# The first k tiles of a fused attention and feed-forward kernel: maxima ahead of transposes, half of the first moves on GpSimd, key sums in their usual beats

## Chip, cores and metric

The kernel runs on one core of a Trainium2 chip. The metric is the device time of one execution in microseconds (us), lower is better. Engines are named as in the profile: PE is TensorE, PEld its weight loads, DVE is VectorE, ACT is ScalarE, POOL is GpSimd, SP is SyncE (it only issues transfers here); a q behind a name (SPq, POOLq) means the engine's queue.

## What is computed

For each of 16 batch items, x is 128 rows by 1024 columns and ctx is the same size. Cut to what matters here:

```python
q = layernorm(x); k = v = ctx
qh = softmax(Wq @ q, over the 64 rows of a head) * 64 ** -0.5
kh = softmax(Wk @ k, over the 1024 columns)        # 8 heads x 64 rows = 4 tiles of 128 rows
context = kh @ vh.T                                # per head, 64 x 64
out = Wo @ (context.T @ qh) + bo
x = x + out / norm(out) * g * sqrt(128)
# then a feed-forward part with a router over 256 slots (aux_keys, aux_values, Wvd, Wvu, Wr)
rk = aux_keys @ Wr.T;  values = aux_values @ Wvd.T # tables, once per call
```

## The kernel before

The attention part is a hand-written software pipeline. A loop `for b in range(PERIODS)` runs over periods, and each engine has its own copy of it with its instructions written out in order; semaphores join the engines. In period b the k side of item b is made (four k tiles, `k_tile(b, i)`, i = 0 to 3, called k(b,i) below), the q side of item b-1 (`q_pair`, `q_shift`, `q_turn`), and the output of item b-2 (`o_pair`). The four values of i are the beats of a period.

One k tile goes through the engines so. PE makes it in PSUM with six products (each operand is split in a high and a low part, so `ctx_hi`, `ctx_lo`, `xn_hi`, `xn_lo` have to be there first). DVE takes its maximum (`k_maximum`, tile `nkm`), ACT takes the exponential (`k_exponential`, `ek`), DVE transposes it in 32 x 32 blocks (`k_turn`, `kt`). In period 0 the tiles use two PSUM places in turn, `k_slot` and `q_slot`, so k(0,2) waits for the exponential of k(0,0) and k(0,3) for that of k(0,1); later k tiles share `k_slot` alone, and k(1,0) waits for the exponential of k(0,3).

When two tiles of an item are transposed, 16 small transfers of 64 KB (`move_k(b, half)`, SBUF to SBUF, 32 partitions by 2 by 256 elements each) put the blocks in `ekT`. PE then sums keys times context over 8 steps (`g_part(b, half, ...)` into `gm`), ACT copies the sum (`g_copy`), PE multiplies by the head products (`m_product`), ACT scales (`mt_scale`).

The q side: `q_pair(b, i)` makes two row blocks in `q_slot`; DVE takes maxima (`qm`) and subtracts (`qs_sb`), ACT takes the exponential, DVE sums (`qsum`) and inverts (`qrec`), POOL multiplies (`q_scale`), PE transposes (`q_turn`), ACT copies. `q_pair` of item b also needs `x_low(b)` from POOL. The layernorm of item b takes statistics on DVE (`x_statistics`), a power on POOL (`rstd_pow`), a bias on DVE (`x_bias`, tile `nb`), then ACT (`x_layernorm`, `x_high`) and POOL (`x_low`).

The router tables come by five transfers that POOL issues once, and PE makes two sets of products of them: `value_products` (16 short products, which the trace counts as 32, and one of the router) and `score_product`. DVE order in period 0 is: maximum of tile i-1, transpose of tile i-1, maximum of tile i, so the maximum of a tile stands behind the transpose of the one before.

Of the kernel before, what the change touches and what calls it, by code (L numbers as in the profile page):

```python
# [47 lines left out]
def attention_ffn_kernel(nc, x, ctx_rows, ctx_cols, WqT_raw, WkT_raw, Wv_rows, WoT_rows, bo_row, g_col, Wuq_cols,  # L48
# [3 lines left out]
    with ctx:  # L52
# [207 lines left out]
        k_T = sem("k_T")  # L260
        k_moved = [sem(f"k_moved{k}") for k in range(2)]
        krec_done = sem("krec_done")
        kscale_done = sem("kscale_done")
# [84 lines left out]
        def has(b):  # L348
            return 0 <= b < B

        @block.sync
        def _(sp):
# [12 lines left out]
            def move_k(b, half):  # L365

                sp.wait_ge(k_T, 4 * b + 2 * half + 2)
                wait(sp, g_prod, 2 * (b - 1) + half + 1)
                for q in range(QUAD):
                    for a in range(QUAD):  # L370
                        sp.dma_start(ekT[q * BLK:(q + 1) * BLK, 2 * half:2 * half + 2, a, :],
                                     kt[a * BLK:(a + 1) * BLK, 2 * half:2 * half + 2,
                                        q * J * BLK:(q + 1) * J * BLK]).then_inc(k_moved[half], 16)
# [24 lines left out]
            for half in range(2):  # L398
                sp.wait_ge(k_moved[half], MOVED * B)
            sp.dma_start(Wuq_in[:, :, :], Wuq_cols).then_inc(wuq_in, 16)  # L400
# [24 lines left out]
        def _(pe):  # L425
# [33 lines left out]
            def g_part(b, half, js):  # L459

                if js[0] == 0:
                    pe.wait_ge(k_moved[half], MOVED * (b + 1))
                    if half == 0:
                        pe.wait_ge(ctxT_in[b % 2], 16 * (b // 2 + 1))
                        wait(pe, mt_copied, b)
                cols = slice(half * 2 * P, (half + 1) * 2 * P)
                for j in js:
                    last = nc.tensor.matmul(gm[:, cols], ctxT[:, b % 2, j, :], ekT[:, 2 * half:2 * half + 2, :, j * BLK:(j + 1) * BLK],  # L468
                                            start=(j == 0), stop=(j == J - 1))
                if js[-1] == J - 1:  # L470
                    last.then_inc(g_prod, 1)
# [37 lines left out]

            def value_products():  # L510
                pe.wait_ge(table_in, 16 * TABLES)
                for s in range(NSLOT // P):
                    for j in range(J):
                        last = nc.tensor.matmul(ob[:, s * VB:(s + 1) * VB], valuesT[:, j, s * P:(s + 1) * P],
                                                WvdT[:, j, :], start=(j == 0), stop=(j == J - 1))
                last.then_inc(vv_prod, 1)
                nc.tensor.matmul(ob[0:RDIM, NSLOT:2 * NSLOT], WrT, keysT, start=True, stop=True).then_inc(rk_prod, 1)

# [87 lines left out]
            for b in range(PERIODS):  # L606
                p, o, e = b - 1, b - 2, b - 3
                for i in range(4):
                    if has(b):
                        k_tile(b, i)  # L610
                    qb, qi = (p, i - 2) if i >= 2 else (o, i + 2)
                    if has(qb):
                        if qb == 0 and qi == 0:
                            pe.wait_ge(u_done, 1)
                            pe.wait_ge(ident_in, 16)
                        take_turn(q_turn, qb, qi)
                        q_turn(qb, qi)
# [83 lines left out]
        def _(act):  # L701
# [102 lines left out]
            for weights, raw, come, done in ((WkT, WkT_in, k_weights_in, k_weights),  # L804
# [3 lines left out]
                if weights is WkT:  # L808
                    ctx_high(0)
            x_layernorm(0)  # L810
            x_high(0)
            for b in range(PERIODS):
                p, o, e = b - 1, b - 2, b - 3
                for i in range(4):
# [7 lines left out]
                    if has(qb):  # L822
                        q_exponential(qb, qi)
                    if has(b):
                        k_exponential(b, i)
                    if i == 1 and has(b + 1):
                        ctx_high(b + 1)
# [12 lines left out]
                    if i == 2:  # L840
                        if has(p) and p > 0:
                            g_copy(p)
                        if 0 < b < B:
                            x_high(b)
                    if b == 1 and i == 0:
                        act.wait_ge(u_prod, 1)
                        nc.scalar.copy(U[:, :, :].rearrange("p h c -> p (h c)"), turn[:, :]).then_inc(u_done, 1)
                    if b == 1 and i == 3:
                        g_copy(0)
                        act.wait_ge(vv_prod, 1)  # L850
                        nc.scalar.copy(VV[:, :, :].rearrange("p s (r d) -> p s r d", d=VB),
                                       ob[:, 0:2 * VB].rearrange("p (s d) -> p s d", d=VB).unsqueeze(2).broadcast_to(
                                           [P, NSLOT // P, P // VB, VB])).then_inc(vv_copied, 1)
                        act.wait_ge(rk_prod, 1)
# [4 lines left out]
                    if b == 2 and i == 0:  # L859
                        act.wait_ge(b1_prod, 1)  # L860
# [5 lines left out]
                    if b == B and i == 3:  # L866
                        for half in range(2):
                            act.wait_ge(k_moved[half], MOVED * B)
                        h_scale(0, 0)
# [50 lines left out]
        def _(pool):  # L920
# [52 lines left out]
            nc.gpsimd.memset(scoreB[BOT:P, :], 0.0).then_inc(score_zeros, 1)  # L973
            pool.wait_ge(score_zeros, 1)
            rstd_pow(0)
            x_low(0)
            ctx_low(1)
            nc.gpsimd.dma_start(valuesT, values_cols).then_inc(table_in, 16)
            nc.gpsimd.dma_start(WvdT, Wvd_cols).then_inc(table_in, 16)
            nc.gpsimd.dma_start(keysT, keysT_raw).then_inc(table_in, 16)  # L980
            nc.gpsimd.dma_start(WrT, WrT_raw).then_inc(table_in, 16)
            nc.gpsimd.dma_start(Wr_in, Wr_raw).then_inc(table_in, 16)
            for n in range(2):
                nc.gpsimd.dma_start(scoreB[BOT:BOT + 1, n * NSLOT:(n + 1) * NSLOT], log_rel_row).then_inc(log_rel_in, 16)
            for b in range(PERIODS):
                p, o, e = b - 1, b - 2, b - 3
                for i in range(4):
# [15 lines left out]
                    if b == B and i == 3:  # L1003
                        for half in range(2):
                            pool.wait_ge(k_moved[half], MOVED * B)
                        nc.gpsimd.memset(q_rows[:, :, BOT:P], 1.0).then_inc(query_ones, 1)
# [29 lines left out]
        def _(dve):  # L1036
# [21 lines left out]
            def k_turn(b, i):  # L1058
                dve.wait_ge(k_exp, 4 * b + i + 1)
                wait(dve, k_moved[i // 2], MOVED * b)  # L1060
                V.transpose(kt[:, i, :], ek[:, i % 2, :]).then_inc(k_T, 1)  # L1061
# [144 lines left out]
            def hidden_step(b):  # L1206
                if b == 0:
                    dve.wait_ge(ffn_in, 16 * FFN_DMAS)
                    for half in range(2):
                        dve.wait_ge(k_moved[half], MOVED * B)  # L1210
                    hT_low(0, 0)
# [37 lines left out]
            weights_low(WqT, WqT_in, q_weights)  # L1249
            x_bias(0)  # L1250
            for b in range(PERIODS):
                p, o, e = b - 1, b - 2, b - 3
                for i in range(4):
                    kb, ki = (b, i - 1) if i else (p, 3)
                    if has(kb):
                        k_turn(kb, ki)
                    if has(b):
                        k_maximum(b, i)
# [130 lines left out]
```

## Time and profile before

| what | value |
|---|---|
| median of 3 runs | 663.33 us (662.93 to 663.96) |
| the profiled execution, its own time | 663.27 us |
| its span, first to last instruction | 661.5 us |
| PE busy | 625.1 us, 95% |
| DVE busy | 579.0 us, 88% |
| ACT busy | 419.5 us, 63% |
| POOL busy | 366.4 us, 55% |

The span is 1.8 us shorter than the time of the same execution; the difference lies outside the first and last instruction. Busy shares are averages over the attention part, the feed-forward part and the two ends, so they don't say what holds any one stretch.

### The profile page before, as it was taken

What the parts mean: (1) busy time and instruction counts of PE and PEld (TensorE: products, weight loads), DVE (VectorE), ACT (ScalarE), POOL (GpSimd) and SP (SyncE); (2) the same over time, 40 slices, a digit from 0 to 9 for tenths busy, and PEclk for the clock granted to TensorE, in tenths of its full rate; (3) what the DMA queues carried; (4) which work ended last, traced back from release to release, by engine and by line L of the source; (5) the groups of instructions that cost most, each with busy time, mean ns of one, the idle gap of its engine ahead of it and who ended that gap; (6) DMA issues with size and microseconds to landing.
All of it is one profiled execution on the core that took longest, in us unless ns stands there. A gap on an engine that the chain in (4) does not pass through costs nothing.

```text
span 661.5 us, 11769 instructions
## 1 busy us (share of the span) xinstructions
PE 625.1 (95%) x3974; PEld 546.4 (83%) x3974; DVE 579.0 (88%) x788; ACT 419.5 (63%) x844; POOL 366.4 (55%) x275
## 2 busy tenths in 40 slices
PE   4699999999999999999999999999999799999896
PEld 2487888888888888888888888888889799998574
DVE  4697899999999999999999999999997656866897
ACT  4355676666666666666666766666573856584784
POOL 2434355565655647464646565656546576752294
PEclk9799999999999999999999999999999899999898
DMA  7644244434434343434343434443234100000056
GB/s 262 190 122 121 81 143 112 144 86 143 124 100 133 102 133 102 135 96 136 101 136 104 133 97 134 123 130 97 65 101 148 41 1 2 1 1 1 33 209 268
DMA packets 52779, 72.57 MB, mean 110 GB/s; under 512 B 10112, under 2 KB 43424, under 8 KB 52464
## 3 DMA queue, kind: packets, MB, share of 16 engines
q1 hardware_dynamic: 52336, 70.43, 35.6%
q0 software_dynamic: 384, 1.40, 0.7%
q8 instruction: 32, 0.52, 0.4%
q14 instruction: 27, 0.22, 0.1%
HBM read 29.85 MB, written 8.39 MB: 58 GB/s over the span
## 4 chain that ended last, share of the span: by engine, by line
PE 45%; DVE 29%; issue 19%; ACT 3%; DMA 2%; SPq 2%; POOL 1%; DVEq 0%; ACTq 0%; POOLq 0%
PE gm L468 9%; DVE qm L1075 7%; DVE qsum L1085 7%; PE ob L491 6%; PE gm L542 4%; PE turn L542 4%; DVE nkm L1056 3%; DVE qs_sb L1078 3%; DVE st L1042 3%; DVE st L1100 3%; PE q_slot L428 2%; PE turn L499 2%; DVE kt L1061 2%; PE k_slot L428 2%; PE k_slot L430 2%
## 5 line engine op out<-in xcount | busy, mean ns | idle before, releaser
L942 POOL TENSOR_TENSOR qs_sb<-qs_sb,qrec 128x1024 f32<-128x1024 f32 x64 | 122.0, 1907 | 211.6 <-DVE qrec L1089 211.6
L723 ACT ACTIVATE ek<-k_slot,nkm 128x1024 f32<-128x1024 f32 x62 | 69.1, 1114 | 104.4 <-DVE nkm L1056 104.4
L491 PE MATMUL ob<-mt_sb,q_hd 128*128 128x128 f32 x1024 | 127.3, 278 | 3.7 <-POOL mt_sb L948 3.1
L491 PEld LDWEIGHTS ob<-mt_sb,q_hd 128*128 128x128 f32 x1024 | 122.5, 193 | 8.4 <-issue 3.5
L468 PE MATMUL gm<-ekT,ctxT 128*128 128x256 f32 x512 | 118.2, 379 | 0.0
L468 PEld LDWEIGHTS gm<-ekT,ctxT 128*128 128x128 f32 x512 | 97.0, 190 | 14.8 <-DMA ekT<-kt 0.3
L733 ACT ACTIVATE qs_sb<-qs_sb 128x1024 f32<-128x1024 f32 x64 | 68.5, 1070 | 42.4 <-DVE qs_sb L1078 42.4
L1056 DVE TENSOR_REDUCE nkm<-k_slot 128x1 f32<-128x1024 f32 x62 | 74.2, 1197 | 17.6 <-PE k_slot L430 17.6
L1061 DVE STREAM_TRANSPOSE kt<-ek 128x1024 f32<-128x1024 f32 x64 | 78.6, 1228 | 5.8 <-ACT ek L723 5.8
L1085 DVE TENSOR_REDUCE qsum<-qs_sb 128x16 f32<-128x1024 f32 x64 | 76.9, 1202 | 5.2 <-ACT qs_sb L733 5.2
L1078 DVE TENSOR_TENSOR qs_sb<-q_slot,qm 128x1024 f32<-128x1024 f32 x64 | 78.4, 1225 | 2.2
L1075 DVE TENSOR_REDUCE qm<-q_slot 128x16 f32<-128x1024 f32 x64 | 75.3, 1177 | 0.0
L428 PE MATMUL k_slot<-ctx_hi,WkT_hi 128*128 128x512 f32 x124 | 55.1, 445 | 13.1 <-DVE ctx_lo L1246 7.4
L454 PE MATMUL turn<-ident,qs_sb 128*128 128x128 f32 x512 | 66.3, 273 | 0.0
L454 PEld LDWEIGHTS turn<-ident,qs_sb 128*128 128x128 f32 x512 | 59.6, 141 | 7.8
L738 ACT COPY q_hd<-turn 128x1024 f32<-128x1024 f32 x64 | 64.3, 1005 | 2.0 <-PE turn L454 2.0
L428 PE MATMUL q_slot<-WqT_hi,xn_hi 128*128 128x512 f32 x128 | 55.8, 436 | 6.1 <-DVE qs_sb L1078 5.2
L429 PE MATMUL q_slot<-WqT_hi,xn_lo 128*128 128x512 f32 x128 | 50.6, 396 | 0.0
L430 PE MATMUL q_slot<-WqT_lo,xn_hi 128*128 128x512 f32 x128 | 50.6, 396 | 0.0
L430 PE MATMUL k_slot<-ctx_lo,WkT_hi 128*128 128x512 f32 x124 | 50.1, 404 | 0.0
L429 PE MATMUL k_slot<-ctx_hi,WkT_lo 128*128 128x512 f32 x124 | 49.6, 400 | 0.0
L968 POOL TENSOR_TENSOR x_all<-x_all,hbuf 128x1024 f32<-128x1024 f32 x16 | 38.7, 2428 | 9.8 <-ACT hbuf L770 9.8
(195 smaller groups left out, 1270.7 us busy)
## 6 DMA issues: line engine op xcount, KB each, us to landing
ekT<-kt SPq DMA_DIRECT2D x512, 64.0 KB, 2.0
ctx_in<-ctx_rows SPq DMA_DIRECT2D x16, 512.0 KB, 4.6
x_all<-x SPq DMA_DIRECT2D x16, 512.0 KB, 3.6
ctxT<-ctx_cols SPq DMA_DIRECT2D x16, 512.0 KB, 4.0
out<-q_hd SPq DMA_DIRECT2D x15, 512.0 KB, 2.6
Wuq_in<-Wuq_cols SPq DMA_DIRECT2D x1, 1280.0 KB, 5.4
x_all<-values_cols POOLq DMA_DIRECT2D x1, 1024.0 KB, 6.1
WvuT_in<-WvuT_raw SPq DMA_DIRECT2D x1, 512.0 KB, 4.6
```

The costliest lines, as they stand in the source:

```text
L428: nc.tensor.matmul(dst, lhs[0], rhs[0], start=True, stop=False)
L429: nc.tensor.matmul(dst, lhs[1], rhs[0], start=False, stop=False)
L430: return nc.tensor.matmul(dst, lhs[0], rhs[1], start=False, stop=True)
L454: last = nc.tensor.transpose(turn[:, (2 * t + n) * P:(2 * t + n + 1) * P], qs_sb[:, i % 2, n * HALF + t * P:n * HALF + (t + 1) * P], ident ...
L468: last = nc.tensor.matmul(gm[:, cols], ctxT[:, b % 2, j, :], ekT[:, 2 * half:2 * half + 2, :, j * BLK:(j + 1) * BLK], start=(j == 0), stop ...
L491: last = nc.tensor.matmul(ob[:, (j % 4) * C:(j % 4 + 1) * C], q_hd[:, t, j * P:(j + 1) * P], mt_sb[:, b % 2, t, :], start=(t == 0), stop=( ...
L942: nc.gpsimd.tensor_tensor(e, e, qrec[:, i % 2, :].unsqueeze(2).broadcast_to([P, PAIR, DH]), ALU.mult).then_inc(q_mul, 1)
L1056: V.tensor_reduce(nkm[:, i:i + 1], k_psum(b, i)[:, :], AX, ALU.max, negate=True).then_inc(k_max, 1)
L1061: V.transpose(kt[:, i, :], ek[:, i % 2, :]).then_inc(k_T, 1)
L1075: V.tensor_reduce(qm[:, :], q, AX, ALU.max).then_inc(q_max, 1)
L1078: V.tensor_tensor(qs_sb[:, i % 2, :].rearrange("p (m d) -> p m d", d=DH), q, qm[:, :].unsqueeze(2).broadcast_to([P, PAIR, DH]), ALU.subtra ...
L1085: V.tensor_reduce(qsum[:, :], qs_sb[:, i % 2, :].rearrange("p (m d) -> p m d", d=DH), AX, ALU.add).then_inc(q_sum, 1)
```

## The change

On DVE the four maxima and three of the four transposes of item 0 are written ahead of the loop, each maximum ahead of the transpose of the tile before. ACT's first exponentials stand between the layernorm, `ctx_high(1)` and `x_high(0)`. POOL issues the table transfers first, then makes `ctx_low(1)` and `x_low(0)`, then issues 8 of the 16 moves of each half of item 0; SP issues the other 8. The key sums of item 0 (`g_part`) go to the beats that all other items have, the value products are split in two and moved ahead, and the copies of the tables on ACT are moved with them.

```diff
 sync:    def move_k(b, half):
                 for q in range(QUAD):
-                    for a in range(QUAD):
+                    for a in range(QUAD // 2 if b == 0 else QUAD):
 tensor:  def g_part(b, half, js):
-                    pe.wait_ge(k_moved[half], MOVED * (b + 1))
+                    pe.wait_ge(k_moved[half], moved(b + 1))
+                    if b == 0:
+                        pe.wait_ge(k_moved_first[half], MOVED // 2)
...
+                    if b == 1 and i == 1:
+                        value_products(1)
+                        router_product()
...
-                        if p == 0 and i == 1:
-                            g_part(p, 0, range(0, 8))
-                        if p == 0 and i == 3:
-                            g_part(p, 1, range(0, 8))
+                        if p == 0 and i == 0:
+                            value_products(0)
-                        if p > 0 and i == 1:
-                            g_part(p, 0, range(4, 8))
-                        if p > 0 and i == 2:
+                        if i == 1:
+                            g_part(p, 0, range(4 if p > 0 else 0, 8))
+                        if i == 2:
                             g_part(p, 1, range(0, 8))
...
                     if b == 1 and i == 2:
-                        value_products()
-                    if b == 1 and i == 3:
                         score_product()
 scalar:      x_layernorm(0)
+            k_exponential(0, 0)
+            ctx_high(1)
+            k_exponential(0, 1)
             x_high(0)
+            k_exponential(0, 2)
+            k_exponential(0, 3)
...
                     if i == 2:
-                        if has(p) and p > 0:
+                        if has(p):
                             g_copy(p)
...
-                    if b == 1 and i == 3:
-                        g_copy(0)
-                        act.wait_ge(vv_prod, 1)
+                    if b == 1 and i == 1:
+                        act.wait_ge(vv_prod, NSLOT // P)
+                        act.wait_ge(rk_prod, 1)
 gpsimd:
+            def move_k(half):
+                pool.wait_ge(k_T, 2 * half + 2)
+                for q in range(QUAD):
+                    for a in range(QUAD // 2, QUAD):
+                        nc.gpsimd.dma_start(ekT[...], kt[...]).then_inc(k_moved_first[half], 16)
             rstd_pow(0)
-            x_low(0)
-            ctx_low(1)
             (five table transfers)
+            ctx_low(1)
+            x_low(0)
+            for half in range(2):
+                move_k(half)
             (two transfers of log_rel)
 vector:      x_bias(0)
+            k_maximum(0, 0)
+            for i in range(1, 4):
+                k_maximum(0, i)
+                k_turn(0, i - 1)
```

In the rows of instruction order below, the line numbers of before and after differ, since the file has grown. On DVE at the start of the program, `nkm` is a k tile's maximum and `kt` its transpose. Before:

```order
L1056 TENSOR_REDUCE nkm<-k_slot 128x1
L1061 STREAM_TRANSPOSE kt<-ek 128x1024
L1056 TENSOR_REDUCE nkm<-q_slot 128x1
L1061 STREAM_TRANSPOSE kt<-ek 128x1024
L1056 TENSOR_REDUCE nkm<-k_slot 128x1
```

And now, at the same place on DVE:

```order
L1078 TENSOR_REDUCE nkm<-k_slot 128x1
L1078 TENSOR_REDUCE nkm<-q_slot 128x1
L1085 STREAM_TRANSPOSE kt<-ek 128x1024
L1078 TENSOR_REDUCE nkm<-k_slot 128x1
L1085 STREAM_TRANSPOSE kt<-ek 128x1024
```

The second maximum has gone ahead of the first transpose, and so on down the four tiles. On POOL at the start of the program (DMA is the issue of a transfer), before:

```order
L932 TENSOR_TENSOR rstd<-ve,half_neg 128x1
L936 TENSOR_TENSOR xn_lo<-xn,xn_hi 128x1024
L923 TENSOR_TENSOR ctx_lo<-ctx_in,ctx_hi 128x1024
L978 DMA x_all<-values_cols 128x2048
L979 DMA x_all<-Wvd_cols 128x512
L980 DMA x_all<-keysT_raw 64x256
L981 DMA x_all<-WrT_raw 64x48
L982 DMA x_all<-Wr_raw 48x64
L984 DMA scoreB<-log_rel_row 1x16x16 x2
L930 TENSOR_SCALAR ve<-mv 128x1
```

And now on POOL:

```order
L944 TENSOR_TENSOR rstd<-ve,half_neg 128x1
L996 DMA x_all<-values_cols 128x2048
L997 DMA x_all<-Wvd_cols 128x512
L998 DMA x_all<-keysT_raw 64x256
L999 DMA x_all<-WrT_raw 64x48
L1000 DMA x_all<-Wr_raw 48x64
L935 TENSOR_TENSOR ctx_lo<-ctx_in,ctx_hi 128x1024
L948 TENSOR_TENSOR xn_lo<-xn,xn_hi 128x1024
L991 DMA ekT<-kt 32x2x256 x16
L1006 DMA scoreB<-log_rel_row 1x16x16 x2
L942 TENSOR_SCALAR ve<-mv 128x1
```

The two subtractions changed places and stand behind the tables, and 16 issues of moves stand ahead of the power for item 1's layernorm (`ve<-mv`). On PE, from the end of the q pair of beat 2 of period 1 to k(1,3), before:

```order
L430 MATMUL q_slot<-WqT_lo,xn_hi 128x512
L514 MATMUL ob<-x_all 128x64 x16
L517 MATMUL ob<-x_all 48x256
L428 MATMUL k_slot<-ctx_hi,WkT_hi 128x512
L429 MATMUL k_slot<-ctx_hi,WkT_lo 128x512
```

And now the same part of period 1 on PE (`ob<-x_all 128x64` are the value products, `48x256` the router's, `64x256` the score product, `gm` the key sums):

```order
L436 MATMUL q_slot<-WqT_lo,xn_hi 128x512
L476 MATMUL gm<-ekT,ctxT 128x256 x8
L531 MATMUL ob<-x_all 64x256
L434 MATMUL k_slot<-ctx_hi,WkT_hi 128x512
L435 MATMUL k_slot<-ctx_hi,WkT_lo 128x512
```

The second half of the key sums now stands ahead of k(1,3), where the value products were; those stand around k(1,1), eight products ahead of it and eight behind.

## Rows read from the trace of the kernel before

**Rows 1.** Chain of work that ended last: start us, us, engine, tile, line.

```profile
42.57 3.52 PE ob L514 x32
46.09 0.56 PE ob L517 x2
...
54.62 1.09 PE gm L477 x16
...
104.34 3.45 PE gm L468 x16
```

**Rows 2.** Stretches, each engine's busy us, PEclk the granted clock.

```profile
24.00:27.00 3.00, 2.23 (x5) 1.82 (x6) 1.25 (x1) 0.63 (x2) 0.58 (x2) 0.50 0.95 342
...
56.00:86.00 30.00, 30.00 (x192) 26.12 (x191) 26.08 (x29) 19.26 (x36) 11.38 (x9) 1.00 0.33 90
```

**Rows 3.** Timeline of period 0: start us, us, engine line op, then idle before.

```profile
10.38 1.23 DVE L1056 TENSOR_REDUCE nkm<-k_slot 128x1 f32<-128x1024 f32 x1 [0.16 <-PE k_slot L430]
...
12.27 0.63 PE L430 MATMUL q_slot<-ctx_lo,WkT_hi 128*128 128x512 f32 x1
12.55 1.11 ACT L723 ACTIVATE ek<-k_slot,nkm 128x1024 f32<-128x1024 f32 x1
...
13.78 1.25 DVE L1061 STREAM_TRANSPOSE kt<-ek 128x1024 f32<-128x1024 f32 x1 [2.17 <-ACT ek L723]
...
13.89 0.47 PE L428 MATMUL k_slot<-ctx_hi,WkT_hi 128*128 128x512 f32 x1 [0.99 <-ACT ek L723]
...
14.95 1.19 DVE L1056 TENSOR_REDUCE nkm<-q_slot 128x1 f32<-128x1024 f32 x1
...
24.77 0.76 PE L428 MATMUL k_slot<-ctx_hi,WkT_hi 128*128 128x512 f32 x1 [4.54 <-ACT ek L723]
```

**Rows 4.** Timeline: issues of transfers on the queues of SP and POOL.

```profile
8.24 0.43 SPq L384 DMA_DIRECT2D ident<-identity  x1
...
18.68 10.60 SPq L371 DMA_DIRECT2D ekT<-kt  x16
...
20.69 0.81 POOL L978 DMA_DIRECT2D x_all<-values_cols  x1
...
22.04 0.56 POOL L980 DMA_DIRECT2D x_all<-keysT_raw  x1
```

**Rows 5.** Transfers of the first 60 us: KB each, median us from issue to landing.

```profile
ekT<-kt SPq DMA_DIRECT2D x57, 64.0 KB, 2.0
...
x_all<-keysT_raw POOLq DMA_DIRECT2D x1, 64.0 KB, 6.3
```

**Rows 6.** Timeline of period 1, first half, DVE and one PE row.

```profile
27.70 1.22 DVE L1056 TENSOR_REDUCE nkm<-k_slot 128x1 f32<-128x1024 f32 x1 [1.80 <-PE k_slot L430]
...
36.55 1.87 DVE L1051 SCALAR_TENSOR_TENSOR nb<-mv,rstd 128x1 f32<-128x1 f32 x1
...
39.59 1.23 DVE L1078 TENSOR_TENSOR qs_sb<-q_slot,qm 128x1024 f32<-128x1024 f32 x1
...
40.96 0.47 PE L428 MATMUL q_slot<-WqT_hi,xn_hi 128*128 128x512 f32 x1 [0.74 <-DVE qs_sb L1078]
```

**Rows 7.** Timeline from beat 3 of period 1 into period 2.

```profile
46.58 0.50 PE L428 MATMUL k_slot<-ctx_hi,WkT_hi 128*128 128x512 f32 x1
...
48.08 1.03 PE L454 MATMUL turn<-ident,qs_sb 128*128 128x128 f32 x8
...
48.28 1.22 DVE L1056 TENSOR_REDUCE nkm<-k_slot 128x1 f32<-128x1024 f32 x1 [0.30 <-PE k_slot L430]
...
48.87 0.48 PE L428 MATMUL q_slot<-WqT_hi,xn_hi 128*128 128x512 f32 x1
...
50.33 3.61 PE L468 MATMUL gm<-ekT,ctxT 128*128 128x256 f32 x16
...
52.85 2.36 POOL L936 TENSOR_TENSOR xn_lo<-xn,xn_hi 128x1024 fp32r<-128x1024 f32 x1
...
58.51 0.48 PE L428 MATMUL q_slot<-WqT_hi,xn_hi 128*128 128x512 f32 x1
```

More of the change, by code:

```diff
@@ L261, in attention_ffn_kernel @@
         k_moved = [sem(f"k_moved{k}") for k in range(2)]
+        k_moved_first = [sem(f"k_moved_first{k}") for k in range(2)]
         krec_done = sem("krec_done")
@@ L349, in has, with moved @@
             return 0 <= b < B
+        def moved(b):
+            return MOVED * b - MOVED // 2 if b else 0
         @block.sync
@@ L398, in _ @@
             for half in range(2):
-                sp.wait_ge(k_moved[half], MOVED * B)
+                sp.wait_ge(k_moved[half], moved(B))
             sp.dma_start(Wuq_in[:, :, :], Wuq_cols).then_inc(wuq_in, 16)
@@ L508, in head_products, with value_products, router_product @@
                 last.then_inc(u_prod, 1)
-            def value_products():
+            def value_products(s):
                 pe.wait_ge(table_in, 16 * TABLES)
[L512 to L515, printed above, removed]
+                for j in range(J):
+                    last = nc.tensor.matmul(ob[:, s * VB:(s + 1) * VB], valuesT[:, j, s * P:(s + 1) * P],
+                                            WvdT[:, j, :], start=(j == 0), stop=(j == J - 1))
                 last.then_inc(vv_prod, 1)
+            def router_product():
                 nc.tensor.matmul(ob[0:RDIM, NSLOT:2 * NSLOT], WrT, keysT, start=True, stop=True).then_inc(rk_prod, 1)
@@ L823, in _ @@
                         q_exponential(qb, qi)
-                    if has(b):
+                    if 0 < b < B:
                         k_exponential(b, i)
-                    if i == 1 and has(b + 1):
+                    if i == 1 and 0 < b and has(b + 1):
                         ctx_high(b + 1)
@@ L853, in _ @@
                                            [P, NSLOT // P, P // VB, VB])).then_inc(vv_copied, 1)
-                        act.wait_ge(rk_prod, 1)
                         nc.scalar.copy(rkT, ob[0:RDIM, NSLOT:2 * NSLOT]).then_inc(rk_copied, 1)
@@ L858, in _ @@
                                       float(BOT) ** -0.5).then_inc(score_ready, 1)
-                    if b == 2 and i == 0:
+                    if b == 1 and i == 3:
                         act.wait_ge(b1_prod, 1)
@@ L867, in _ @@
                         for half in range(2):
-                            act.wait_ge(k_moved[half], MOVED * B)
+                            act.wait_ge(k_moved[half], moved(B))
                         h_scale(0, 0)
@@ L974, in _ @@
             pool.wait_ge(score_zeros, 1)
+            def move_k(half):
+                pool.wait_ge(k_T, 2 * half + 2)
+                for q in range(QUAD):
+                    for a in range(QUAD // 2, QUAD):
+                        nc.gpsimd.dma_start(ekT[q * BLK:(q + 1) * BLK, 2 * half:2 * half + 2, a, :],
+                                            kt[a * BLK:(a + 1) * BLK, 2 * half:2 * half + 2,
+                                               q * J * BLK:(q + 1) * J * BLK]).then_inc(k_moved_first[half], 16)
             rstd_pow(0)
-            x_low(0)
-            ctx_low(1)
             nc.gpsimd.dma_start(valuesT, values_cols).then_inc(table_in, 16)
@@ L1004, in _ @@
                         for half in range(2):
-                            pool.wait_ge(k_moved[half], MOVED * B)
+                            pool.wait_ge(k_moved[half], moved(B))
                         nc.gpsimd.memset(q_rows[:, :, BOT:P], 1.0).then_inc(query_ones, 1)
@@ L1059, in k_turn @@
                 dve.wait_ge(k_exp, 4 * b + i + 1)
-                wait(dve, k_moved[i // 2], MOVED * b)
+                wait(dve, k_moved[i // 2], moved(b))
+                if b == 1:
+                    dve.wait_ge(k_moved_first[i // 2], MOVED // 2)
                 V.transpose(kt[:, i, :], ek[:, i % 2, :]).then_inc(k_T, 1)
@@ L1209, in hidden_step @@
                     for half in range(2):
-                        dve.wait_ge(k_moved[half], MOVED * B)
+                        dve.wait_ge(k_moved[half], moved(B))
                     hT_low(0, 0)
@@ L1254, in _ @@
                     kb, ki = (b, i - 1) if i else (p, 3)
-                    if has(kb):
+                    if has(kb) and b > 0:
                         k_turn(kb, ki)
-                    if has(b):
+                    if 0 < b < B:
                         k_maximum(b, i)
```

## The prediction

> **What bounds the kernel now.** I read the chain of work that ended last first. From about 42 us on it runs through PE for two periods and keeps coming back to it: value products, key sums, head products [rows 1]. The table of stretches says the same of period 2: in the 30.00 us from 56 to 86, PE is busy for all 30.00 and DVE for 26.08, so PE holds and DVE waits [rows 2]. So what counts is how early PE gets into period 2 and how early the k and q chains feed it; from there on, as long as nothing else is late, every microsecond won at the start is won at the end. The timeline of period 0 shows a different picture: there the tiles go round one by one. A tile's maximum stands behind the transpose of the tile before (13.78, then 14.95) although its product was finished at 12.27 + 0.63 = 12.90 [rows 3], and PE sits idle for 4.54 us ahead of k(1,0) at 24.77 [rows 3]. The stretch that follows has a granted clock of 0.50 [rows 2], that is 1.2 GHz of the levels 1.2 and 2.4.
>
> **Period 0, step by step.** Four handovers are read from rows 3: maximum to exponential 1.22 (10.38 + 1.23, about when the next may start), exponential to transpose 13.78 - 12.55 = 1.23, exponential to the next k tile on PE 13.89 - 12.55 = 1.34, transpose to what follows on DVE 14.95 - 13.78 = 1.17 [rows 3]; what follows a maximum on DVE starts 1.12 later (27.70 to the next at 28.85 is 1.15). A k tile's maximum starts 48.28 - 46.58 = 1.70 after the tile [rows 7]. Maximum 0 stays at 10.38, and exponential 0 moves to 11.60, since ACT's cast goes behind it. Maximum 1 starts at 12.94, when its product is done. k(0,2) starts at 11.60 + 1.34 = 12.94. DVE: transpose 0 at 14.06, maximum 2 at 15.23, transpose 1 at 16.35, maximum 3 at 17.51, transpose 2 at 18.63. ACT: exponential 1 at 12.94 + 1.22 = 14.16, 2 at 16.45, 3 at 18.73; the casts `ctx_high(1)` and `x_high(0)`, about 1 us each, lie in the holes between and cost nothing (12.8 to 13.8, and 15.4 to 16.4); without those holes each would cost its 1 us. Transpose 3 follows at about 20.0, and k(1,0) starts at 18.73 + 1.34 = 20.07 in place of 24.77: **4.7 us** earlier. PE's idle time ahead of it falls from 4.54 to about 2 us. A gap of that size in period 0 (idle between k(0,2) and k(0,3)) was not followed by a fall of the clock, so I count k(1,0) and the first q pair at 2.4 GHz. If the clock fell all the same, the 12 products at 1.2 GHz would cost up to 2.3 us more.
>
> **POOL's queue.** This is the part with a price that the trace doesn't show. `rstd_pow(0)` ends near 10.0, five table issues follow (0.81 for the first, 0.56 for the others [rows 4]) to about 13.0, `ctx_low(1)` is done at 16.3 and `x_low(0)` at 16.5 + 2.4 = 18.9, both ahead of 20.07. The tables have from about 12.5 to 23 us to land. Then come 16 issues of moves of unknown price p, two issues for `log_rel` (about 1.0 together) and the power (0.9): item 1's `rstd` is ready at 20.75 + 16p. Behind it wait DVE's `nb`, and behind that all of DVE. For p the nearest row is the issue of `keysT_raw`, also 64 KB and also 64 runs of 1 KB: 0.56 [rows 4]. The far bounds are 0.81, the dearest POOL issue, and 0.56 x 0.66/0.43 = 0.86, if this shape costs POOL as much more as it costs SP: 10.60/16 = 0.66 for a move, 0.43 for the 64 KB of `ident` [rows 4]. I take 0.56, by likeness of the transfer: `rstd` at 29.7. DVE takes the maximum of k(1,0) at 20.07 + 1.70 = 21.8 and reaches `nb` 36.55 - 27.70 = 8.85 later [rows 6], at 30.6. So 0.9 us is in hand, and `nb` costs nothing extra. With 0.81 or 0.86 DVE waits 3.1 or 3.9 us.
>
> The same rows bear on contention: beside the table issues, from 21.0 to 23.4, DVE did a transpose and a maximum, and the issue in their midst kept its 0.56 [rows 4]. So I count no hindrance. If DVE's transposes and statistics between 19 and 29 us (four instructions or pairs, 1.25 for a transpose [rows 3]), did hold POOL up for their length, `rstd` would come 5 us later.
>
> The Trainium skill ("SBUF — State Buffer", the warning on the DVE that blocks DMA, section "SBUF: two separate sides") states that GpSimd cannot write descriptors while a DVE instruction in a two-port mode holds the port pair they share. If the transposes and statistics were of that kind, that would be the case of the 5 us; the trace's 0.56 beside a transpose speaks against it.
>
> **Landing of the moves.** DVE wants half 0 moved for the transpose of k(1,0), PE for the key sums. SP issues its 8 of half 0 from 17.6 (end of transpose 1) to 22.9, POOL its 8 from 18.9 to 23.3. Landing takes 2.0 at the median for a move, 6.3 for POOL's 64 KB table [rows 5]; that one stood behind a table of 1 MB on the same queue, and nothing of that size is ahead of the moves now, so I take 3. Half 0 is there at about 26. The transpose is due at 26.7 and the key sums at 30: nothing lost. With 6.3 it is there at 29.1, a DVE wait of 2.4. Half 1 is issued by 28.8 on SP and 27.8 on POOL and wanted at 37 or later.
>
> **Period 1 on PE.** Now it should run almost without a hole. From k(1,0) to k(1,3) stand three k tiles at 1.50, three q pairs at 1.46, one transpose at 0.79 [rows 7], two key sums at 3.45, the value products at 3.52, router and score product at 0.56 each [rows 1]: 4.50 + 4.38 + 0.79 + 6.90 + 3.52 + 1.12 = 21.2, so k(1,3) starts at 41.3. Waits that could break it: q pair 2 needs the subtraction of pair 1, 3.04 behind `nb` plus 1.37 [rows 6], 30.6 + 4.4 = 35.0, and PE comes there at 35.8, so 0.8 us in hand; the value products wait for the tables, landed; the key sums for the moves, landed; ACT's copies of the tables (1.1 us together) stand behind the layernorm that ends near 33.6 and ahead of an exponential due at 34.9, so they just fit.
>
> **What is given back.** The next q pair (item 1, pair 0) needs `x_low(1)` on POOL, and that follows k(1,3)'s maximum by way of DVE's sum and POOL's scaling: from the maximum to the end of `x_low`, 52.85 + 2.36 - 48.28 = 6.93 [rows 7]. So this pair starts at 41.3 + 1.70 + 6.93 = 49.9. PE itself would be there at 41.3 + 1.5 + 0.8 + 1.5 + 1.1 (`m_product` [rows 1]) + 1.5 + 0.8 = 48.4; 1.5 us of PE's lead is lost to POOL. Before, the same pair started at 58.51 [rows 7]. 58.5 - 49.9 = 8.6, and I count **8.5 us**: 4.7 from period 0, 5.3 from holes and slow products in period 1, 1.5 given back. DVE is then ahead by about 8.8, SP's moves by 5 or more where they had slack, so none of them is the later one, and PE keeps the lead through period 2, which had no hole [rows 2]. Against the profiled execution: 663.27 - 8.5 = **654.8**; the median of before is within 0.1 of it.
>
> **The rivals.** (1) *POOL's issues are dear.* A wait w of DVE at `nb` reaches PE as w - 0.8. With p = 0.81 the gain is 8.5 - 2.3 = 6.2, time 657.1; with 0.86, 657.9; with 5 us of hindrance by DVE, w = 5.0 - 0.9 = 4.1, 658.1 (0.04 of the chance). For it: the move is of a shape that costs SP half as much again. Against: the 64 KB row at 0.56. (2) *Moves land late:* DVE waits 2.4 at the transpose of k(1,0), 2.4 - 0.8 = 1.6 pass on: 656.4. For it: 6.3 us in rows 5, and two queues now move at once; against: no 1 MB ahead. (3) *The clock:* slow products at k(0,2) cost 0.6 and at k(1,0) up to 2.3: 655.4 to 657.1. (4) *Slower than before:* the issues of moves hold POOL so long that the power for item 1 comes later than all that was won. That needs w - 0.8 over 8.5, w = 9.3, so 20.75 + 16p = 39.9, p = 1.2. At p = 1.3, w = 10.95 and the time is 663.3 + 1.6 = 664.9. The dearest issue in sight is 0.86, so the chance is small. (5) *The later beats don't gain:* only period 0's 4.7 arrives because ACT's copies or the value products delay the q chain as much as the holes were worth: 658.6. Against: the slack of 0.8 and 1.3 us worked out above. (6) *Absorbed:* were DVE or SP the bound of the later periods, little would come through; rows 2 speak against it, time 662 to 663.3.
>
> **How the numbers follow.** Forecast as summed 0.56; (1) 0.20; (2) 0.07; (3) 0.06; (4) 0.03; (5) 0.04; (6) 0.04. The forecast alone has a range of 653.7 to 656.0, from handovers that are good to 0.1 each over some ten steps. To hold 8 in 10, the range takes in (1) up to 0.86 with some blocking, (2), (3) and (5): 653.6 to 658.8. A measurement of this kernel tells about 0.2%, 1.3 us, from no change. Faster 0.92, within 0.2% 0.04, slower 0.04.
>
> **What would show it.** The maximum of k(0,1) starts near 12.9 and k(1,0) near 20.1, with products of 0.39 and not 0.63. POOL's 16 issues take about 9 us, and `nb` of item 1 starts near 30.6 with no wait for POOL. The transpose of k(1,0) starts near 26.7 with no wait for a move. PE's q pair of item 1 starts near 49.9 and waits about 1.5 us for `xn_lo`. The end is 8.5 us earlier, all of it won before 60 us, and later periods as long as before. It is wrong if POOL's issues take over 0.66 each, if DVE waits for `ekT` moves, or if the lead shrinks between period 2 and the end.

## The result and the profile after

| | median (runs) | ratio to before, 95% interval |
|---|---|---|
| before | 663.64 us (4) | |
| changed kernel | 655.15 us (4; 653.82 to 656.4) | 0.987 [0.9846, 0.9895] |
| changed kernel, once more | 655.35 us (6; 653.69 to 658.12) | 0.9877 [0.9858, 0.9897] |

The change saves 8.5 us. The profiled execution took 655.03 us with a span of 653.2, so 8.24 less than that of before. Timeline of the changed kernel, DVE and PE in period 0 and the first half of period 1 (the answer to [rows 3] and [rows 6]):

```profile
11.35 1.22 DVE L1078 TENSOR_REDUCE nkm<-k_slot 128x1 f32<-128x1024 f32 x1
12.48 1.22 DVE L1078 TENSOR_REDUCE nkm<-q_slot 128x1 f32<-128x1024 f32 x1
13.90 1.25 DVE L1085 STREAM_TRANSPOSE kt<-ek 128x1024 f32<-128x1024 f32 x1 [0.20 <-ACT ek L731]
...
14.01 0.47 PE L434 MATMUL k_slot<-ctx_hi,WkT_hi 128*128 128x512 f32 x1 [1.72 <-ACT ek L731]
...
20.54 0.47 PE L434 MATMUL k_slot<-ctx_hi,WkT_hi 128*128 128x512 f32 x1 [1.79 <-ACT ek L731]
...
27.12 1.24 DVE L1085 STREAM_TRANSPOSE kt<-ek 128x1024 f32<-128x1024 f32 x1
...
31.03 1.87 DVE L1073 SCALAR_TENSOR_TENSOR nb<-mv,rstd 128x1 f32<-128x1 f32 x1
```

The second maximum follows the first at once, PE's idle time ahead of k(1,0) is 1.79 us where it was 4.54, and neither the transpose of k(1,0) nor `nb` has a wait. The queues, in the timeline of the changed kernel (answer to [rows 4]):

```profile
11.18 0.80 POOL L996 DMA_DIRECT2D x_all<-values_cols  x1
...
12.53 0.54 POOL L998 DMA_DIRECT2D x_all<-keysT_raw  x1
...
19.55 8.46 POOL L991 DMA_DIRECT2D ekT<-kt  x16
27.99 1.01 POOL L1006 DMA_DIRECT2D scoreB<-log_rel_row  x2
...
29.36 0.58 POOL L944 TENSOR_TENSOR rstd<-ve,half_neg 128x1 f32<-128x1 f32 x1
...
18.07 5.22 SPq L377 DMA_DIRECT2D ekT<-kt  x8
```

A move costs POOL 8.46 / 16 = 0.53 us and SP 5.22 / 8 = 0.65. Transfers of the first 60 us (answer to [rows 5]), then the two stretches of [rows 2], then PE from k(1,3) on (answer to [rows 7]):

```profile
ekT<-kt SPq DMA_DIRECT2D x48, 64.0 KB, 2.0
...
ekT<-kt POOLq DMA_DIRECT2D x16, 64.0 KB, 3.8
```

```profile
24.00:27.00 3.00, 3.00 (x23) 2.74 (x22) 2.93 (x5) 1.57 (x3) 3.00 (x7) 1.00 0.94 215
...
56.00:86.00 30.00, 30.00 (x194) 26.45 (x194) 27.22 (x31) 20.26 (x42) 13.50 (x9) 1.00 0.44 128
```

```profile
41.65 0.50 PE L434 MATMUL k_slot<-ctx_hi,WkT_hi 128*128 128x512 f32 x1
...
46.51 0.50 PE L434 MATMUL k_slot<-ctx_hi,WkT_hi 128*128 128x512 f32 x1
...
50.34 0.50 PE L434 MATMUL q_slot<-WqT_hi,xn_hi 128*128 128x512 f32 x1 [1.17 <-POOL xn_lo L948]
```

The granted clock from 24 to 27 us is 1.00, where it was 0.50; PE is full in period 2 as before; and item 1's first q pair starts at 50.34 in place of 58.51, after a wait of 1.17 for `xn_lo`. That is 58.51 - 50.34 = 8.17 us won by 51 us. At the end of the attention part nothing of it is lost. DVE's `nb` there, of the changed kernel and of before:

```profile
492.63 1.87 DVE L1131 SCALAR_TENSOR_TENSOR nb<-mv,rstd 128x1 f32<-128x1 f32 x1
```

```profile
500.87 1.87 DVE L1107 SCALAR_TENSOR_TENSOR nb<-mv,rstd 128x1 f32<-128x1 f32 x1
```

500.87 - 492.63 = 8.24, and the two executions differ by 8.24. I use this `nb`, "the late `nb`", as the mark for all runs below, since what follows it differs between executions of one kernel (last section).

### The profile page after: what moved, and what is told of

It reads as the page before. It is cut to its first block, busy times and chain, and to the rows that moved or that the text cites. A ratio compares the mean times of both kernels' runs of the same rounds, so it can differ in the third digit from the quotient of the medians.

```text
span 653.2 us, 11771 instructions
## 1 busy us (share of the span) xinstructions
PE 621.8 (95%) x3974; PEld 544.4 (83%) x3974; DVE 578.9 (89%) x788; ACT 419.2 (64%) x844; POOL 374.8 (57%) x291
## 4 chain that ended last, share of the span: by engine, by line
PE 43%; DVE 29%; issue 20%; ACT 3%; DMA 2%; SPq 2%; POOL 2%; DVEq 0%; ACTq 0%; POOLq 0%
PE gm L476 8%; DVE qsum L1109 7%; DVE qm L1099 7%; PE ob L499 7%; PE gm L551 4%; PE turn L551 4%; DVE nkm L1078 3%; DVE st L1064 3%; DVE qs_sb L1102 3%; DVE st L1124 3%; PE turn L507 2%; PE q_slot L434 2%; PE k_slot L434 2%; PE k_slot L436 2%; DVE kt L1085 2%
```

## Experiments

### The parts alone and in pairs

The change has three parts: the maxima ahead of transposes (with ACT's new order), POOL's part (tables early, half of the moves), and the beats (key sums, value products, copies). Six kernels were made of combinations of them.

**start_only**: the kernel before with the maxima and ACT's order alone (and `ctx_low(1)` ahead of `x_low(0)` on POOL, as ACT's order wants it).

```diff
 vector:  k_maximum(0, 0)
+         for i in range(1, 4):
+             k_maximum(0, i)
+             k_turn(0, i - 1)
 scalar:  k_exponential(0, 0); ctx_high(1); k_exponential(0, 1); x_high(0); ...
```

> Period 0 alone: maxima ahead of transposes on DVE, ACT's early exponentials, ctx_low(1) ahead of x_low(0) on GpSimd; but all moves on SyncE, the tables issued behind both, and the beats of period 1 as before. Theory A (the parts need each other: in the kernel before, half 0 of the moves landed near 32.5 us, just when the transpose of k(1,0) stood at its turn at 32.64): k(1,0) starts near 20.5, but that transpose still waits for SyncE's moves until about 32, and the gain over the kernel before is 1 us or less: 662.5 to 663.4. Rival R (whatever brings k(1,0) forward comes through whole): gain 4 to 7 us, 656.5 to 659.5.

**sp_moves**: the changed kernel with all 16 moves of each half on SP; POOL issues only the tables, early.

```diff
-                    for a in range(QUAD // 2 if b == 0 else QUAD):
+                    for a in range(QUAD):
...
 gpsimd:
-            for half in range(2):
-                move_k(half)
```

> The changed kernel with all 16 moves of each half of item 0 on SyncE again, GpSimd issuing only tables. Theory A: half 0 is issued from 18.1 to 28.7 and lands at 30.7 to 31.5, the transpose of k(1,0), due at 27.1, waits about 3.6 to 4.4; half 1 lands near 42 and the second key sums wait for it too: together 3 to 4.5 us slower than the changed kernel, 658.2 to 659.7. Rival R: the moves were hidden anyway, 655.2.

**old_beats**: the changed kernel with PE's and ACT's orders of key sums, value products and copies as before.

```diff
-                        if p == 0 and i == 0:
-                            value_products(0)
+                        if p == 0 and i == 3:
+                            g_part(p, 1, range(0, 8))
...
+                    if b == 1 and i == 2:
+                        value_products()
```

> The changed kernel with the value products, the key sums of item 0 and ACT's copies of both in their old beats. Theory A: PE then waits about 2.4 and 0.9 for DVE's subtractions where the value products stood, but k(1,3) starts about as early (41.0 against 41.65), and the second sums, their copy and the score product behind it put PE's q pair of item 1 near 51.3 against 50.34: 1.0 us slower than the changed kernel, 656.2. Rival B (the beats are what fills PE's holes, worth 3 us or more): 658 or more.

**beats_only**: the kernel before with the new beats alone (the same lines the other way round).

> The kernel before with only the beats of period 1 changed (value products split and ahead, key sums and copies in their usual beats). Theory A: period 0 and the moves stay as they are, the second half of the sums waits for moves issued until 40.2 and landed near 43, k(1,3) starts near 48.7 in place of 46.6, and the q pair of item 1 near 57.4 in place of 58.5: 1.1 us faster than before, 662.5. Rival B: 3 us or more faster, 660.5 or less.

**old_maxima**: the changed kernel with each maximum behind the transpose of the tile before; ACT's order stays new.

```diff
             for i in range(1, 4):
-                k_maximum(0, i)
                 k_turn(0, i - 1)
+                k_maximum(0, i)
```

> The changed kernel with DVE's maxima of item 0 behind the transposes again, everything else as changed. Theory A: the tiles of period 0 go round at 3.6 us each again, k(1,0) starts near 24.2 in place of 20.5, PE has stood idle for more than 4 us ahead of it and its first 12 products run at 1.2 GHz, which costs DVE's maximum another 1.2: 4.5 to 5.5 us slower than the changed kernel, 659.7 to 660.7. Rival (the moves on GpSimd and the beats do the work, the maxima are hidden): within 1 us of 655.2.

**pool_only**: the kernel before with POOL's part alone.

```diff
             rstd_pow(0)
-            x_low(0)
-            ctx_low(1)
             (five table transfers)
+            ctx_low(1)
+            x_low(0)
+            for half in range(2):
+                move_k(half)
...
```

> The kernel before with POOL's part of the change alone: tables issued ahead of ctx_low(1) and x_low(0), and half of item 0's moves on POOL. Maxima, ACT's order and the beats as before. Theory A (the moves only matter when the transpose of k(1,0) comes early): before, that transpose at 32.6 us had no wait, so nothing is won: 663.6, within 0.5, and POOL's last moves end near 33.4, its power for item 1 near 35.3, still ahead of nb at 36.5. Rival B (the parts add up, and POOL's part is worth what it is worth in the whole change, 3.4 us): 660.2. Rival C: POOL's issues delay the power for item 1, and DVE waits at nb: 665 or more.

Measured. The gain is the difference of medians to the runs of before beside them (663.85 us at the median for start_only, beats_only, sp_moves and old_beats, 663.66 for old_maxima, 663.75 for pool_only), ratios with their intervals; the last two columns are the starts of two DVE instructions in each kernel's profile:

| kernel | maxima | POOL | beats | median us | ratio | gain | transpose of k(1,0) | late `nb` |
|---|---|---|---|---|---|---|---|---|
| before | | | | 663.64 | | | 32.64 | 500.87 |
| start_only | x | | | 661.48 | 0.9963 [0.995, 0.9976] | 2.4 | 30.71 | 498.9 |
| pool_only | | x | | 663.62 | 0.9998 [0.9989, 1.0007] | 0.1 | 32.69 | 500.9 |
| beats_only | | | x | 662.07 | 0.9971 [0.9959, 0.9984] | 1.8 | 32.73 | 499.3 |
| sp_moves | x | tables only | x | 658.54 | 0.9913 [0.9886, 0.994] | 5.3 | 31.11 | 496.3 |
| old_beats | x | x | | 657.7 | 0.9903 [0.9881, 0.9926] | 6.1 | 25.98 | 494.1 |
| old_maxima | ACT only | x | x | 660.49 | 0.9957 [0.9945, 0.997] | 3.2 | 31.86 | 498.0 |
| changed | x | x | x | 655.15 | 0.987 [0.9846, 0.9895] | 8.5 | 27.12 | 492.63 |

Alone the parts give 2.4 + 0.1 + 1.8 = 4.3, together 8.5: half of the gain is in none of them. Most of the reason stands in two rows. Timeline of DVE in start_only and in sp_moves:

```profile
30.71 1.25 DVE L1080 STREAM_TRANSPOSE kt<-ek 128x1024 f32<-128x1024 f32 x1 [4.11 <-DMA ekT<-kt]
```

```profile
31.11 1.25 DVE L1079 STREAM_TRANSPOSE kt<-ek 128x1024 f32<-128x1024 f32 x1 [4.27 <-DMA ekT<-kt]
```

With the maxima early and all moves on SP, k(1,0) is on PE at 19.93 or 20.17, 4.6 us or more ahead of before, and DVE then stands 4.1 to 4.3 us for the moves: SP's 16 issues of a half take 10.3 us in either. start_only did as the theory of late moves says as to that wait, though its 2.4 is more than the 1 us at most that I gave it: SP could start on the moves at 17.47 in place of 18.68, and the transpose came at 30.71, not near 32 as expected. POOL's part removes just this wait: worth nothing alone (pool_only), where DVE came to the transpose at 32.69 with no wait, and 8.5 - 5.3 = 3.2 us (sp_moves against the changed kernel) once DVE comes early. sp_moves has a granted clock of 1.00 from 24 to 56 us, so this 3.2 is no matter of the clock.

The beats need POOL's part too. Alone (beats_only) they gain 1.8, where 1.1 was expected, and the value products in their new place wait for a table that is still issued late, as the timeline of PE shows:

```profile
30.00 2.00 PE L513 MATMUL ob<-x_all 128*128 128x64 f32 x16 [0.92 <-DMA x_all<-Wr_raw]
```

In pool_only POOL was done even earlier than I wrote (moves at 31.51 where I had 33.4, the power at 33.46 where I had 35.3):

```profile
23.06 8.45 POOL L986 DMA_DIRECT2D ekT<-kt  x16
31.51 1.01 POOL L1001 DMA_DIRECT2D scoreB<-log_rel_row  x2
32.54 0.25 POOL L937 TENSOR_SCALAR ve<-mv 128x1 f32<-128x1 f32 x1
32.88 0.58 POOL L939 TENSOR_TENSOR rstd<-ve,half_neg 128x1 f32<-128x1 f32 x1
```

old_maxima costs 5.3 of the 8.5, as expected: its k(1,0) starts at 24.35, as before. old_beats costs 2.4, and 1.0 was expected. Its idle times on PE (timeline) say where the rest is:

```profile
23.66 0.47 PE L434 MATMUL k_slot<-ctx_hi,WkT_hi 128*128 128x512 f32 x1 [1.27 <-ACT ek L731]
26.20 0.47 PE L434 MATMUL q_slot<-WqT_hi,xn_hi 128*128 128x512 f32 x1 [0.94 <-DVE qs_sb L1103]
34.28 0.47 PE L434 MATMUL q_slot<-WqT_hi,xn_hi 128*128 128x512 f32 x1 [0.74 <-DVE qs_sb L1103]
```

```profile
39.92 0.50 PE L434 MATMUL k_slot<-ctx_hi,WkT_hi 128*128 128x512 f32 x1
...
47.96 1.09 PE L485 MATMUL gm<-U,g_sb 128*64 128x128 f32 x16 [0.68 <-ACT g_sb L737]
...
51.85 0.47 PE L434 MATMUL q_slot<-WqT_hi,xn_hi 128*128 128x512 f32 x1
```

1.27 + 0.94 + 0.74 + 0.68 = 3.63 against the changed kernel's one wait of 1.17 in the same stretch, 2.46 more: the size of the 2.4. The new beats put half of the value products into the hole ahead of k(1,1), and the key sums into the others. The forecast of 1.0 went wrong behind k(1,3): that tile starts 20.5 us behind k(1,0) at 19.39, as expected (41.0 against 20.54), but from there to item 1's q pair it took 51.85 - 39.92 = 11.93, and 51.3 - 41.0 = 10.3 was expected.

### The two terms of the prediction that rest on POOL

**pool_late**: the changed kernel with five writes of zeros (1.00 us each) into a tile not yet in use, on POOL between the moves and `log_rel`.

```diff
             for half in range(2):
                 move_k(half)
+            for _ in range(5):
+                if _:
+                    pool.wait_ge(late, _)
+                nc.gpsimd.memset(o_sb[:, 0, :, :], 0.0).then_inc(late, 1)
```

> The changed kernel with five memsets of about 1 us, each waiting for the one before, on GpSimd behind its 16 issues of moves: stands for dearer issues. Theory A (slack of 1.1 us at nb, then 0.8 on PE): rstd of item 1 comes about 5.2 later, at 35.1, nb waits about 4.1, PE's q pair of item 1 is 3.3 later: 658.5. Rival (the layernorm of item 1 is far from the path): 655.2.

Measured: 658.55 us, ratio 0.9927 [0.9904, 0.995], 3.4 over the changed kernel. Timeline of DVE, and below it the landing times of the moves in pool_late (view of the tile `ekT`, 17 to 36 us):

```profile
28.13 1.25 DVE L1090 STREAM_TRANSPOSE kt<-ek 128x1024 f32<-128x1024 f32 x1 [1.83 <-DMA ekT<-kt]
...
33.90 1.87 DVE L1078 SCALAR_TENSOR_TENSOR nb<-mv,rstd 128x1 f32<-128x1 f32 x1 [1.76 <-POOL rstd L945]
```

```profile
DMA to landing us min/median/max: 2.9/5.8/7.9
```

The size is as forecast, and `nb` does wait for POOL. But in this execution the transpose had waited 1.83 for moves already, so the two waits share the delay: 1.83 + 1.76 = 3.6. The five writes take 5.01 us, and `rstd`, at 33.86, is later than it would be by as much, so 5.0 - 3.6 = 1.4 was DVE's slack, where the prediction had 0.9. From k(1,0) to k(1,3) PE took 43.88 - 19.63 = 24.25, 3.1 more than the 21.11 of the changed kernel, so PE's slack was about 0.5, where the prediction had 0.8. Their sum is as taken (1.9 against 1.7), the two parts are not. PE's first wait, too, is for POOL's scaling of a q pair, which stands behind the same writes, and not for DVE (timeline of PE):

```profile
35.89 1.06 PE L461 MATMUL turn<-ident,qs_sb 128*128 128x128 f32 x8 [1.10 <-POOL qs_sb L955]
```

The late `nb` is at 494.85.

### The clock in the kernel before

**warm_before**: the kernel before with the head products made four times over, to keep PE busy ahead of k(1,0).

```diff
-                for h in range(H):
+                for h in list(range(H)) * 4:
```

> The kernel before with the 8 head products of period 0 done four times over, so that PE works through the gap ahead of k(1,0). Theory A: the first 12 products of period 1 run at 2.4 GHz, the maximum of k(1,0) starts 1.2 earlier, but the transpose of k(1,0) waits for its moves until about 32.6 as before: at most 0.3 us faster, 663.3. Rival C (the clock term comes through): 1.2 to 2.3 us faster, 661.3 to 662.4.

Measured: 664.99 us, ratio 1.002 [1.0008, 1.0031]; profiled 663.1. Timeline of PE and DVE in warm_before:

```profile
19.48 4.89 PE L506 MATMUL turn<-q_hd 64*128 64x128 f32 x64
...
24.66 0.47 PE L428 MATMUL k_slot<-ctx_hi,WkT_hi 128*128 128x512 f32 x1 [0.29 <-ACT ek L723]
```

```profile
26.31 1.23 DVE L1056 TENSOR_REDUCE nkm<-k_slot 128x1 f32<-128x1024 f32 x1 [0.52 <-PE k_slot L430]
...
32.48 1.25 DVE L1061 STREAM_TRANSPOSE kt<-ek 128x1024 f32<-128x1024 f32 x1 [1.16 <-DMA ekT<-kt]
```

From 24 to 56 us the granted clock is 1.00. The products of k(1,0) are at 2.4 GHz (0.47 for the first, against 0.76 [rows 3]), and its maximum starts 1.39 us earlier than in [rows 6]. DVE then gives it back in a new wait of 1.16 for the moves, and the transpose is at 32.48 where it was 32.64. So in the kernel before the clock hid behind the moves and cost nothing by itself; the late `nb` is at 500.8, as before. The time itself is not as expected (at most 0.3 faster): the median is 1.3 us slower than the runs of before beside it and 1.9 above the profiled execution, which is the fastest of the ten. Why stays open.

### The wait for x_low

**x_low_early**: the changed kernel with `x_low(b)` ahead of `q_scale` in beat 3, for every item.

```diff
 gpsimd, beat 3:
+                    if i == 3 and 0 < b < B:
+                        x_low(b)
                     if has(qb):
                         q_scale(qb, qi)
-                    if i == 3 and 0 < b < B:
-                        x_low(b)
```

> The changed kernel with x_low(b) ahead of q_scale on GpSimd in beat 3 of every period. Theory A: the 1.2 us that PE waits for xn_lo at 50.3 go away, but DVE is only 0.4 us ahead of PE there, so 0.2 to 0.5 faster than the changed kernel: 654.8. Rival (GpSimd alone took back the lead): 1.2 us faster, 654.0. Rival (the order of all later periods was tuned to the old place): slower.

**x_low_again** (the same kernel, more rounds), **x_low_item1** (moved for `b == 1` alone) and **after_again** (the changed kernel) ran side by side later.

> The earlier kernel with x_low ahead of q_scale for every item, once more with more rounds, beside the changed kernel. Theory A (its two new waits on PE in the last attention period are there every time): 0.3 to 0.8 under the changed kernel. Rival B (what the first look showed was the low clock of one execution after the last attention period, 6.9 us of half clock in place of 3.3): 1.2 to 1.6 under the changed kernel.

> The changed kernel, with x_low moved ahead of q_scale in beat 3 for item 1 alone; all later items as in the changed kernel. In the earlier kernel that moved it for all items, PE got into period 2 without a wait and 1.6 us ahead of the changed kernel at the first layernorm of the feed-forward part, but it had two new waits of 0.5 us each on PE in the last attention period. Theory A (those two and the low clock that follows them took the gain): here the gain of 1.2 to 1.6 at the start stays, and the time is 0.8 to 1.6 under the changed kernel run beside it. Rival B (the late part absorbs it whatever the order): within 0.3 of the changed kernel. Rival C: POOL's q_scale, now 2.4 us later, delays the q chain of item 0 and costs 1 us or more.

> The changed kernel itself, on the same chip and in the same rounds as the three others, to compare them with. 655.2 within 0.8. Between 505 and 525 us, where PE goes from attention to the feed-forward part, its granted clock falls for some us; if that differs from execution to execution, the spread of times is 2 us or more, as in its first runs (653.8 to 656.4), and the intervals up to the first layernorm of the feed-forward part agree within 0.3 us with those of the first profile.

| kernel | median us (runs) | ratio to before | item 1's first q pair | late `nb` |
|---|---|---|---|---|
| after_again | 655.35 (6) | 0.9877 [0.9858, 0.9897] | 49.57, waits 1.17 | 491.8 |
| x_low_early | 655.78 (4) | 0.9885 [0.9854, 0.9916] | 48.00 | 491.0 |
| x_low_again | 654.81 (4) | 0.9862 [0.9849, 0.9876] | 48.52 | 491.4 |
| x_low_item1 | 653.64 (4) | 0.9847 [0.9832, 0.9862] | 47.82 | 490.8 |

Moved for all items it takes the wait away in period 1 and gains nothing that can be told: 0.5 in one comparison, -0.6 in the other. Timelines of PE late in the attention part and after it, of x_low_again and of after_again:

```profile
495.86 0.47 PE L434 MATMUL q_slot<-WqT_hi,xn_hi 128*128 128x512 f32 x1 [0.56 <-DVE qs_sb L1102]
...
509.81 1.06 PE L538 MATMUL k_slot<-ident,hbuf 128*128 128x128 f32 x8 [0.38 <-ACT hbuf L778]
```

```profile
484.80 0.50 PE L434 MATMUL q_slot<-WqT_hi,xn_hi 128*128 128x512 f32 x1 [0.92 <-POOL xn_lo L948]
...
509.81 1.06 PE L538 MATMUL k_slot<-ident,hbuf 128*128 128x128 f32 x8 [0.41 <-ACT hbuf L778]
```

Both are at 509.81 although x_low_again's q pair of the last item had no wait for `xn_lo`: it has two other waits in that period, 0.56 for DVE and 0.29 for a move, in place of the one of 0.92. Moved for item 1 alone, neither is there (the wait for `xn_lo` of the last item is, with 0.93), and PE is at the same product 1.43 us earlier:

```profile
508.38 1.06 PE L538 MATMUL k_slot<-ident,hbuf 128*128 128x128 f32 x8
```

The medians differ by 1.7 (655.35 and 653.64). The start counts for 0.3 of the 1.43 (k(1,0) is at 19.79 and 19.45), and DVE's `qs_sb` takes 0.45 back in period 2. So x_low_item1 is the fastest kernel found, by 1 to 1.7 us; the ratio intervals of it and of after_again just overlap at 0.986, so I don't claim more.

## Why the prediction was right, step by step

- **Period 0.** Said: 12.94 for the second maximum, 20.07 for k(1,0). Measured 12.48 and 20.54, and the first maximum was 0.97 late (11.35 against 10.38), since item 0's load came in later; in after_again k(1,0) is at 19.79. I put the second maximum behind the end of its product, and it stood only behind the first maximum. k(0,2), expected at 12.94, came at 14.01. The term of 4.7 measured 4.23 and 4.98. The late load is in the 8.24 of the profiled execution as well: in after_again the late `nb` is 500.87 - 491.82 = 9.05 ahead of before. That 8.5 was met so closely is in part luck.
- **The clock** stayed at 1.00 with an idle time of 1.79 ahead of k(1,0), as counted.
- **POOL's issue** was taken at 0.56 from `keysT_raw` and is 0.53; `rstd` was ready at 29.94, forecast 29.7. The bounds of 0.81 and 0.86 come from the first, largest table and from SP's ratio; neither carried over. From 24 to 27 us DVE was busy for 2.93 of 3.00 us while POOL issued without a gap, and none of the 16 issues took longer than 0.56. The Trainium skill ("SBUF — State Buffer", "SBUF: two separate sides") has GpSimd held up by a DVE instruction in a two-port mode. None of the transposes, maxima and statistics here did that.
- **Landing** was taken at 3 us for POOL's moves and is 3.8 at the median, 2.2 for the moves issued by 22 us and 4.8 for those of half 1. No wait came of it in this profile, nor in after_again and the three of x_low, but in pool_late, whose program is the same up to the issue of the last move, the transpose waited 1.83 (median 3.3 for POOL's moves issued by 22 us; why they landed later is open). The margin of 0.7 that I worked out is thinner than what landing varies by: rival 2 had 0.07 and came in one of six profiled executions, too few to say that it was underrated. What I misread is [rows 5]: its 2.0 is the median of 57 moves, and the 16 of half 0 among them took 5.0 (next section).
- **Period 1.** k(1,0) to k(1,3) was to take 21.2 and took 41.65 - 20.54 = 21.11. From k(1,0) to item 1's q pair before took 33.74 and now takes 29.80: 3.94 us, against 5.3 - 1.5 = 3.8. Of the 3.94, 2.34 - 1.17 = 1.17 are idle time (before: 0.74 in [rows 6], and the 0.93 and 0.67 of the two rows below, from the timeline of PE before), and the other 2.77 are the same products, the first twelve of them at a higher clock.

```profile
32.87 0.47 PE L428 MATMUL q_slot<-WqT_hi,xn_hi 128*128 128x512 f32 x1 [0.93 <-DVE qs_sb L1078]
...
54.62 1.09 PE L477 MATMUL gm<-U,g_sb 128*64 128x128 f32 x16 [0.67 <-ACT g_sb L729]
```

- **Given back to x_low**: said 1.5, measured 1.17, and x_low_item1 shows that it could be had.
- **Where it ends**: 8.17 us by item 1's q pair, 8.24 at the late `nb` and at the end. No later period took anything, so rival 6 is out; old_beats and the price of issues rule out 5 and 1.

What was wrong is how the sum was told. It reads as if period 0 brought 4.7 and the rest came from period 1, each for itself. The runs show that period 0 brings 2.4 while the moves are on SP, that the moves on POOL bring nothing unless period 0 is early, and that the slow clock cost nothing before (warm_before). The sum came out since it was made for all parts at once.

## What to carry to other kernels

A wait that the profile doesn't show may stand right behind one that it does. Here DVE came to the transpose at 32.64 without a wait, but SP's issues of moves ended at 29.28 [rows 4]. With the median of 2.0 from [rows 5] the last would have landed at 31.3, 1.4 us earlier; the view of the tile `ekT` in the kernel before, from 18 to 29.3 us and then for the last two moves of half 0 alone (28.55 to 29.25 us), says otherwise:

```profile
DMA to landing us min/median/max: 2.0/5.0/7.1
```

```profile
L371 SPq DMA_DIRECT2D ekT<-kt x2: 596/596/597, 28.0 to 28.7; - x2
...
DMA to landing us min/median/max: 3.8/3.8/3.9
```

The last one was issued at 28.7 and landed 3.8 later, at 32.5, so only 0.1 us ahead of the transpose: nothing that is taken out ahead of it comes through unless the moves come earlier as well. Before shortening one chain, list what the others deliver at the same point and when; and before a part is dropped because alone it does nothing, try it with the others. In a steady pipeline, move an instruction for the one item where it waits: moved for all, `x_low` lost all or most of its gain again at the end.

## What the runs showed that I had not expected

The clock falls in some executions just behind the attention part, where PE is idle for about 3.5 of 16 us. The stretch from 508 to 524 us (columns as in [rows 2]) in after_again, the changed kernel's first profile, and x_low_early:

```profile
508.00:524.00 16.00, 12.47 (x102) 11.93 (x101) 10.84 (x13) 11.37 (x25) 13.30 (x10) 1.00 0.16 42
```

```profile
508.00:524.00 16.00, 12.46 (x89) 11.92 (x86) 11.21 (x13) 11.37 (x29) 12.49 (x9) 0.89 0.15 42
```

```profile
508.00:524.00 16.00, 12.34 (x77) 11.97 (x76) 10.13 (x10) 10.27 (x24) 13.38 (x10) 0.79 0.15 42
```

With PE's busy time nearly the same, the granted clock is 1.00, 0.89 or 0.79. From the late `nb` to the end the three took 162.6, 162.4 and 164.2 us: 0.89 costs nothing here. old_beats and pool_late show 0.79 in the same stretch and took 657.38 - 494.13 = 163.3 and 658.30 - 494.85 = 163.5, so 0.79 goes with 0.7 to 1.8 more. Runs of one kernel differ by more (653.69 to 658.12 for the changed kernel). That the clock makes this spread is not shown: of the changed kernel's runs the two fastest (653.69 and 653.82) have the highest mean clocks, 0.999 and 0.997, but 655.41 and 658.12 have the same, 0.992. A difference of 1 us between two kernels is better read at the late `nb` than from single times.

And one 64 KB move costs SP 0.65 us to issue and POOL 0.53, but it lands no later from one than from the other. The 2.0 above is the median of all 48 moves of SP up to 60 us. The transfers of the changed kernel issued from 17 to 29 us:

```profile
ekT<-kt SPq DMA_DIRECT2D x16, 64.0 KB, 3.8
ekT<-kt POOLq DMA_DIRECT2D x16, 64.0 KB, 3.8
```

When a move is issued counts for more than by whom. The 16 of half 0 took 5.0 at the median in the kernel before, with the tables issued from 20.69 on, and 2.0 in sp_moves, where SP issues all of them as well, from 17.63 on, but the tables went out first, from 10.73 on.
